# Splitting the value products of the grouped attention of a two-layer gated Flamingo kernel into three passes

## The chip, the cores and the metric

The kernel runs on one NeuronCore of a Trainium2 chip. It is written in Bass: every engine has a program of its own, which it executes in the order written, and the engines meet only at semaphores. TensorE does the matmuls, VectorE, ScalarE and GpSimd the element-wise work, SyncE issues the DMAs. The metric is the device time of one execution in microseconds (us), as the median of several runs.

## What is computed

The reference is a two-layer network over a batch of 8 sequences of 100 tokens with 256 features. The part that the change touches is the attention inside the second layer's feed-forward block: 32 query heads share 4 heads of keys and values, each 128 wide. Cut to that part:

```python
h = _rmsnorm(hidden_states, ln1_w)
q = (h @ Wq).reshape(B, S, NH, HD)          # NH = 32, HD = 128
k = (h @ Wk).reshape(B, S, KVH, HD)         # KVH = 4
v = (h @ Wv).reshape(B, S, KVH, HD)
q = _rope(q, pos)
k = _rope(k, pos)
k = jnp.repeat(k, rep, axis=2)              # rep = 8
v = jnp.repeat(v, rep, axis=2)
scores = jnp.einsum('bqhd,bkhd->bhqk', q, k) / jnp.sqrt(jnp.float32(HD))
scores = jnp.where(causal[None, None], scores, jnp.float32(-1000000000.0))
attn = jax.nn.softmax(scores, axis=-1)
o = jnp.einsum('bhqk,bkhd->bqhd', attn, v).reshape(B, S, NH * HD) @ Wo
x = resid + o
```

Here S is 100 and B is 8, so there are T = 800 tokens. All of it is in fp32.

## The kernel before, in words

The whole network runs as a row of stages in one launch, with a barrier of all engines between stages. The change lies in the stage of the grouped attention (ST_F in the code). The stages before it compute the first layer, the second layer's first attention and the norms; the stage behind it computes a norm, and then a mixture of experts.

The stage first makes keys and values (PE L2014 and L2019). ScalarE copies the values of each of the 8 sequences from PSUM to the tile `v2` (L1016), and VectorE rotates the keys. Then come 64 units of work. A unit v takes four heads and one sequence: it is 100 query rows by 4 x 100 keys, and its tiles in PSUM are one bank each. Four consecutive units take the same four heads over the four sequences of one half of the batch, eight take the eight heads of a group over one half, and so on over two halves and four groups.

The order of the work is written out by hand as one loop over steps s on every engine, each unit's pieces spread over several steps:

- TensorE, step s: scores of unit s (L2051 writes the mask, L2054 the four heads), the query block s + 6 (L2035 to L2037), an output product that began nine steps earlier (L2091 to L2093), the value product of unit s - 3 (L2073), and the turn (transpose) of the probabilities of unit s - 2 (L2064).
- VectorE, step s: maximum of unit s (L1488) and its subtraction into `d2` (L1492), the low part of the attention output of unit s - 4 (`o2l`, L1514), the sum of unit s - 1 and its reciprocal (L1498, L1500), the two products of the rotation of query block s + 6 (`q2`, L1477, and `qt`, L1481), and in two of eight steps an addition of an output to the residual `R` (L1506).
- ScalarE, step s: the exponential of unit s (L1029), two half copies of query block s + 6 with the halves swapped (`qsw`, L1024 and L1025), the copy of the attention output of unit s - 3 rounded to fp32r (`o2h`, L1047), the copy of the turned probabilities of unit s - 2 out of PSUM (`pt2`, L1036), and in some steps the rounded high part of a block of weights (L1057, L1065).
- GpSimd, step s: the normalisation of unit s - 1 (`p2`, L723), the sum that ends the rotation of query block s + 6 (L717), and in some steps the low part of a block of weights (`wql`, L729, and `wol`, L734).

Products of full precision are done in one of two ways. One is a matmul on fp32 operands, as the value product here. The other splits both operands into a part rounded to fp32r and a rest in fp32r, and sums three matmuls (high by high, high by low, low by high); queries and outputs are done so, and the function `split3` writes it:

```python
mm(out_, wh, mh, start=start, stop=False)
mm(out_, wh, ml, start=False, stop=False)
return mm(out_, wl, mh, start=False, stop=stop)
```

Buffers tie the engines together. The scores have two banks, the turned probabilities one (bank 2), the value product one (bank 3). So the value product of a unit waits until VectorE has made `o2l` of the unit before it, and the turn waits until the turned probabilities of the unit before have left bank 2. Query blocks live in a ring of ten.

Of the kernel before, what the change touches and what calls it, by code (L numbers as in the profile page):

```python
# [9 lines left out]
fp32 = mybir.dt.float32  # L10
fp32r = mybir.dt.float32r
bf16 = mybir.dt.bfloat16
u32 = mybir.dt.uint32
ALU = mybir.AluOpType
ACT = mybir.ActivationFunctionType
# [3 lines left out]
def flamingo(nc, a, out, scratch, sorted_x, sorted_y):  # L19

    P = 128
    B, S, D = a["ctx_T"].shape[0], a["rope_q"].shape[2], a["xT"].shape[0]
    T = B * S
    NC = D // P
    HALF = T // 2
    HB = B // 2
# [26 lines left out]
    G2 = a["L1_ffn_Wk"].shape[1] // P  # L53
    HG = NH2 // G2
    E1 = a["L1_ffn_Wg"].shape[0]
    U0 = B * NC
# [4 lines left out]
    with ctx:  # L61
        def sb(name, shape, dt=fp32, stack=ctx):
            return stack.enter_context(nc.sbuf_tensor(name, shape, dt))
# [6 lines left out]
        hT = sb("hT", [P, NC, T])  # L70
        xc = sb("xc", [P, NC, T])
        sq = sb("sq", [P, NC, T])
        rstd = sb("rstd", [P, T])
# [24 lines left out]
        PS = ctx.enter_context(nc.psum_tensor("PS", [P, 8, 512], fp32))  # L98
# [18 lines left out]
        def moe_memory(tag, stack):  # L117
# [62 lines left out]
        st2 = ExitStack()  # L180
# [9 lines left out]
        qlo = sb("qlo", [P, 2, HALF], fp32r, stack=st2)  # L190
# [21 lines left out]
        QRING = 10  # L212
# [3 lines left out]
        rope2 = sb("rope2", [P, 2, S], stack=st)  # L216
        st2 = ExitStack()
        kr = sb("kr", [P, G2, T], stack=st2)
        v2 = sb("v2", [S, B, G2 * P], stack=st2)
        wq2 = sb("wq2", [P, NC, HG * P], stack=st2)  # L220
        wo2 = sb("wo2", [P, HG, D], stack=st2)
        wqh = sb("wqh", [P, NC, HG * P], fp32r, stack=st2)
        wql = sb("wql", [P, NC, HG * P], fp32r, stack=st2)
        woh = sb("woh", [P, HG, D], fp32r, stack=st2)
        wol = sb("wol", [P, HG, D], fp32r, stack=st2)
        h1h = sb("h1h", [P, NC, T], fp32r, stack=st2)
        h1l = sb("h1l", [P, NC, T], fp32r, stack=st2)
        q2 = sb("q2", [P, QRING, HALF], stack=st2)
        qsw = sb("qsw", [P, 2, HALF], stack=st2)
        qt = sb("qt", [P, 2, HALF], stack=st2)  # L230
        d2 = sb("d2", [S, 3, 4, S], stack=st2)
        p2 = sb("p2", [S, 2, 4, S], stack=st2)
        pt2 = sb("pt2", [S, 2, 4 * S], stack=st2)
        mx2 = sb("mx2", [S, 2, 4], stack=st2)
        su2 = sb("su2", [S, 3, 4], stack=st2)
        sm2 = sb("sm2", [S, 3, 4], stack=st2)
# [31 lines left out]
        p0 = {k: sem(f"l0_{k}") for k in ("q", "k", "ke", "v", "ve", "kx", "o", "vz")}  # L268
        ATT = ("s", "mx", "sub", "exp", "sum", "rec", "norm", "t", "pte", "pv", "pve")
        at = {k: sem(f"att_{k}") for k in ATT}  # L270
# [10 lines left out]
        xa = {k: sem(f"xa_{k}") for k in ("rope", "f", "fe", "fd", "qh", "qhe", "qb", "rp", "rr", "qp",  # L281
                                          "qlo", "qhi", "qst")}
# [3 lines left out]
        fs = {k: sem(f"f_{k}") for k in ("ldk", "k", "kw", "kc", "ka", "v", "ve",  # L286
                                         "ldq", "ldo", "q", "qw", "qc", "qs", "qa", "o", "oa")}
        XQ = 2 * H1
        fs.update(hs=xa["qh"], wqh=xa["qhi"], wql=xa["qlo"], woh=xa["qhe"], wol=xa["qst"], ol=xa["qb"])
        done, stored = sem("done"), sem("stored")  # L290

        block = ctx.enter_context(nc.Block())
# [40 lines left out]
        U2, LEAD, BACK = 2 * B * G2, 6, 9  # L333
# [204 lines left out]
        def _(pool):  # L538
# [174 lines left out]
            def add_queries(n):  # L713

                pool.wait_ge(fs["qs"], n + 1)
                q = q2[:, n % QRING]
                pool.tensor_tensor(q, q, qt[:, n % 2], ALU.add).then_inc(fs["qa"], 1)  # L717

            def normalise2(v):
# [44 lines left out]
        def _(act):  # L764
# [248 lines left out]
                    act.activation(ksw[lo, n % 4], PS[hi, n, 0:HALF], ACT.Copy).then_inc(fs["kw"], 1)  # L1013
            for b in range(B):
                act.wait_ge(fs["v"], b + 1)
                act.activation(v2[:, b, :], PS[0:S, b, :], ACT.Copy).then_inc(fs["ve"], 1)  # L1016

            def swap_queries(n):

# [11 lines left out]
            def keep_turned2(v):  # L1031

                act.wait_ge(at["t"], U0 + v + 1)
                if v >= 2:
                    act.wait_ge(at["pv"], U0 + v - 1)
                act.activation(pt2[:, v % 2], PS[0:S, 2, 0:4 * S], ACT.Copy).then_inc(at["pte"], 1)  # L1036

            def keep_values2(v):

# [69 lines left out]
        def _(dve):  # L1109
# [204 lines left out]
            for u in range(2 * H1 + 2):  # L1314
# [12 lines left out]
                w = u - 2  # L1327
# [78 lines left out]
            for u in range(NU):  # L1406
                k = maximum(u)
            negative_maxima(0, k)
            maxima_rows(0)
            for b in range(B + 1):  # L1410
                for s in range(SP_ if b < B else 15):
# [4 lines left out]
                    if more:  # L1416
                        for u in range(UNITS[s], UNITS[s + 1]):
                            k = maximum(u)
# [37 lines left out]
            def split_inputs(h):  # L1456

                dve.tensor_copy(h1h[:, :, half(h)], h1[:, :, half(h)]).then_inc(fs["hs"], 1)
                dve.wait_ge(fs["hs"], XQ + 2 * h + 1)
                dve.tensor_tensor(h1l[:, :, half(h)], h1[:, :, half(h)], h1h[:, :, half(h)].bitcast(fp32),  # L1460
                                  ALU.subtract).then_inc(fs["hs"], 1)
            split_inputs(0)
            for n in range(2 * G2):
                k_ = kr[:, n // 2, half(n % 2)].rearrange("p (b s) -> p b s", s=S)
                w_, t_ = (t[:, n % 4].rearrange("p (b s) -> p b s", s=S) for t in (ksw, tk))
# [4 lines left out]
                dve.tensor_tensor(k_, t_, w_, ALU.add).then_inc(fs["ka"], 1)  # L1470

            split_inputs(1)

            def rotate_queries(n):

                dve.wait_ge(fs["qw"], 2 * n + 2)
                dve.tensor_tensor(q2[:, n % QRING].rearrange("p (b s) -> p b s", s=S),  # L1477
                                  PS[:, query_bank(n), 0:HALF].rearrange("p (b s) -> p b s", s=S), cq, ALU.mult).then_inc(fs["qc"], 1)
                if n >= 2:
                    dve.wait_ge(fs["qa"], n - 1)  # L1480
                dve.tensor_tensor(qt[:, n % 2].rearrange("p (b s) -> p b s", s=S), qsw[:, n % 2].rearrange("p (b s) -> p b s", s=S),  # L1481
                                  sn, ALU.mult).then_inc(fs["qs"], 1)
# [26 lines left out]
            def low_values2(v):  # L1509

                x, k, b = unit2(v)
                y = 2 * x + k
                dve.wait_ge(at["pve"], U0 + v + 1)
                dve.tensor_tensor(o2l[:, y % 3, :, b % HB, :], PS[:, 3, 0:4 * S].rearrange("p (h s) -> p h s", s=S),  # L1514
                                  o2h[:, y % 3, :, b % HB, :].bitcast(fp32), ALU.subtract).then_inc(fs["ol"], 1)
            for s in range(U2 + BACK + 2):
                if s < U2:
                    shift2(s)
                if 4 <= s < U2 + 4:
                    low_values2(s - 4)  # L1520
                if 1 <= s < U2 + 1:
                    inverse_sum2(s - 1)
                if s + LEAD < U2:
                    rotate_queries(s + LEAD)
                if s >= BACK + 6 and (s - BACK - 6) % HG in (0, 2):
                    add_outputs((s - BACK - 6) // HG, (s - BACK - 6) % HG // 2)
# [34 lines left out]
            for c in range(NC):  # L1561
                for h in range(2):
                    n = 2 * c + h
# [6 lines left out]
        def _(pe):  # L1570
            mm = pe.matmul
# [41 lines left out]
            for c in range(NC):  # L1613
                for h in range(2):
                    mm(PS[:, 4 + c * 2 + h, 0:HALF], wkv0T[:, c * P:(c + 1) * P], c0T[:, half(h)],
                       start=True, stop=True).then_inc(p0["k"], 1)
# [11 lines left out]
            for c in range(NC):  # L1628
                for h in range(2):
                    for i in range(NC):  # L1630
                        last = mm(PS[:, c * 2 + h, 0:HALF], wq0T[:, i, c * P:(c + 1) * P], hT[:, i, half(h)],
                                  start=(i == 0), stop=(i == NC - 1))
# [40 lines left out]
            for c in range(NC):  # L1673
                for h in range(2):
                    for i in range(NC):
                        last = mm(PS[:, c * 2 + h, 0:HALF], wo0T[:, i, c * P:(c + 1) * P], o0T[:, i, half(h)],
                                  start=(i == 0), stop=(i == NC - 1))
# [17 lines left out]
            for b in range(B - 1):  # L1695
                n = B - 1 - b
# [114 lines left out]
            def split3(out_, wh, wl, mh, ml, start, stop):  # L1811
# [4 lines that stand above are left out]
# [54 lines left out]
            for s in range(2 * H1 + 2):  # L1870
                if s < 2 * H1:
                    h, q = s // 2, s % 2
# [167 lines left out]
            def scores2(v):  # L2040

                x, k, b = unit2(v)
                if v == 0:
                    pe.wait_ge(fs["ve"], B)
                if v % HG == 0:
                    pe.wait_ge(fs["ka"], x + 1)
                if v % 4 == 0:
                    pe.wait_ge(fs["qa"], v + 4)
                if v >= 2:
                    pe.wait_ge(at["sub"], U0 + v - 1)  # L2050
                mm(PS[0:S, v % 2, 0:4 * S].rearrange("p (h s) -> p h s", s=S), identb[0:S, 0:S],  # L2051
                   causal[:, None, :].to_broadcast([S, 4, S]), start=True, stop=False)
                for j in range(4):
                    last_ = mm(PS[0:S, v % 2, j * S:(j + 1) * S], q2[:, (HG * x + 4 * k + j) % QRING, b % HB * S:(b % HB + 1) * S],  # L2054
                               kr[:, x // 2, toks(b)], start=False, stop=(j == 3))
                last_.then_inc(at["s"], 1)

            def turn2(v):

                pe.wait_ge(at["norm"], U0 + v + 1)  # L2060
                if v >= 1:
                    pe.wait_ge(at["pte"], U0 + v)
                for j in range(4):
                    last_ = pe.transpose(PS[0:S, 2, j * S:(j + 1) * S], p2[:, v % 2, j, :], ident[0:S, 0:S])  # L2064
                last_.then_inc(at["t"], 1)

            def values2(v):

                x, k, b = unit2(v)
                pe.wait_ge(at["pte"], U0 + v + 1)  # L2070
                if v >= 1:
                    pe.wait_ge(fs["ol"], XQ + v)
                mm(PS[:, 3, 0:4 * S], v2[:, b, x // 2 * P:(x // 2 + 1) * P], pt2[:, v % 2], start=True, stop=True).then_inc(at["pv"], 1)  # L2073

            def outputs2(x, j):

# [123 lines left out]
```

## Time and profile before

| | us |
|---|---|
| median of 3 runs | 1597.94 |
| lowest and highest of them | 1597.33 to 1600.22 |
| the profiled execution, its own time | 1592.69 |
| its span, first to last instruction | 1590.9 |
| TensorE busy in the span | 1476.1 (93%) |
| VectorE busy | 913.4 (57%) |
| ScalarE busy | 619.0 (39%) |
| GpSimd busy | 778.0 (49%) |

All durations below come from the profiled execution. Its time is the span and 1.8 us around it. In the views PE is TensorE, PEld its loading of weights (which overlaps matmuls), DVE VectorE, ACT ScalarE, POOL GpSimd and SP SyncE; an "idle before" names the instruction of another engine whose end released the waiting one. Instructions overlap on an engine: the time from one start to the next is the price that an instruction has in its queue, and can be shorter than its own duration.

### The profile page before, as it was taken

To read this page: it belongs to the slowest core of one execution; us is meant where nothing else is said; L and a number is where in the kernel's file an instruction comes from. 1 tells how busy PE (TensorE), PEld (TensorE's weight loads), DVE (VectorE), ACT (ScalarE), POOL (GpSimd) and SP (SyncE) were. 2 spreads that over 40 slices of the span, in tenths; PEclk is the share of its full clock that TensorE was granted. 3 is DMA by queue.
4 is the path that set the end of the run, shared out by engine and by line. 5 is a ranking of instruction groups with operands and counts; after the bars stand their busy time and mean duration, and the time that the engine had idled before them with its cause. 6 is when DMAs were issued, how large, how long until landed. Compare 5 with 4: busy or idle time off the path is not lost. (4 is left out here: it accounts for less than half of the span.)

```text
span 1590.9 us, 20767 instructions
## 1 busy us (share of the span) xinstructions
PE 1476.1 (93%) x7316; PEld 1108.4 (70%) x7316; DVE 913.4 (57%) x1581; ACT 619.0 (39%) x1116; POOL 778.0 (49%) x605
## 2 busy tenths in 40 slices
PE   7899999899978999999999998979999998899998
PEld 4687466544445766666666665657889887899998
DVE  1662111245556676796787854557778774444444
ACT  2332121133341344343342443356566653333333
POOL 3650102135554897787877855046475651333332
PEclk7896999699997999999999999789999999899999
DMA  8004111611001010110110000200110001344441
GB/s 301 1 1 146 51 44 41 212 48 49 1 8 53 33 57 3 55 57 2 56 57 1 20 1 1 82 27 1 54 43 12 27 1 41 105 122 121 121 121 51
DMA packets 60317, 88.61 MB, mean 56 GB/s; under 512 B 7556, under 2 KB 44612, under 8 KB 60230
## 3 DMA queue, kind: packets, MB, share of 16 engines
q1 hardware_dynamic: 59206, 85.82, 16.8%
q0 software_dynamic: 1024, 1.64, 0.4%
q8 instruction: 53, 0.87, 0.2%
q14 instruction: 34, 0.28, 0.1%
HBM read 81.92 MB, written 5.41 MB: 55 GB/s over the span
## 5 line engine op out<-in xcount | busy, mean ns | idle before, releaser
L966 ACT ACTIVATE prob<-PS 121x800 f32<-121x800 f32 x192 | 158.1, 838 | 256.2 <-PE PS L1949 253.3
L1349 DVE TENSOR_REDUCE mx<-PS 128x1 f32<-128x482 f32 (+1 forms) x312 | 186.0, 651 | 45.8 <-PE PS L1929 44.4
L619 POOL TENSOR_TENSOR e_wl<-e_wf,e_wh 128x768 fp32r<-128x768 f32 x33 | 71.8, 2174 | 174.0 <-ACT e_wh L882 151.8
L1928 PE MATMUL PS<-kth,qs 128*128 128x482 f32 (+1 forms) x312 | 129.6, 415 | 17.9 <-DVE mx L1349 10.2
L696 POOL TENSOR_TENSOR hT<-hT,prob 121x800 f32<-121x800 f32 x56 | 109.5, 1956 | 70.4 <-ACT prob L966 68.4
L1964 PE MATMUL PS<-prob,kvn 121*64 121x400 f32 (+1 forms) x768 | 136.1, 503 | 0.9 <-ACT prob L966 0.9
L696 POOL TENSOR_TENSOR xc<-xc,prob 121x800 f32<-121x800 f32 x56 | 117.1, 2091 | 17.9 <-ACT prob L966 12.5
L1929 PE MATMUL PS<-kl,qm 66*128 66x482 f32 (+1 forms) x312 | 123.6, 396 | 0.0
L1946 PE MATMUL PS<-qs,kth 128*121 128x400 f32 (+1 forms) x384 | 112.1, 374 | 7.9 <-DMA qm<-nml 4.8
L1949 PE MATMUL PS<-qm,kl 66*121 66x400 f32 (+1 forms) x384 | 104.4, 354 | 0.0
L1964 PEld LDWEIGHTS PS<-prob,kvn 121*64 121x64 f32 (+1 forms) x768 | 52.3, 137 | 71.2 <-issue 68.6
L1946 PEld LDWEIGHTS PS<-qs,kth 128*121 128x121 f32 (+1 forms) x384 | 66.0, 189 | 48.2 <-issue 23.8
L1292 DVE TENSOR_TENSOR e_aw<-e_sg,PS 128x400 f32<-128x400 f32 x64 | 36.6, 571 | 102.8 <-ACT e_sg L888 102.8
L1813 PE MATMUL PS<-e_hh,e_wh 128*128 128x400 f32 x264 | 93.4, 354 | 0.3 <-POOL e_wl L619 0.3
L1814 PE MATMUL PS<-e_hl,e_wh 128*128 128x400 f32 x264 | 92.2, 349 | 0.0
L1815 PE MATMUL PS<-e_hh,e_wl 128*128 128x400 f32 x264 | 91.7, 347 | 0.0
L723 POOL TENSOR_TENSOR p<-d,sm 100x400 f32<-100x400 f32 x64 | 54.6, 853 | 75.7 <-DVE sm L1500 74.9
L1928 PEld LDWEIGHTS PS<-kth,qs 128*128 128x128 f32 x312 | 61.6, 197 | 40.8 <-DVE mx L1349 26.3
L717 POOL TENSOR_TENSOR q<-q,qt 128x400 f32<-128x400 f32 x64 | 66.8, 1045 | 46.0 <-DVE qt L1481 46.0
L667 POOL TENSOR_TENSOR rr<-rp 96x400 f32<-96x400 f32 x32 | 32.9, 1028 | 109.2 <-DVE rp L1326 109.2
L888 ACT ACTIVATE e_sg<-PS 128x400 f32<-128x400 f32 x66 | 33.3, 505 | 130.1 <-PE PS L1815 130.1
L1949 PEld LDWEIGHTS PS<-qm,kl 66*121 66x121 f32 (+1 forms) x384 | 72.4, 189 | 0.8
(277 smaller groups left out, 3582.0 us busy)
## 6 DMA issues: line engine op xcount, KB each, us to landing
e_wb<-routing SPq DMA_DIRECT2D x32, 400.0 KB, 4.0
wgu<-in_L_ffn_gate_up_proj SPq DMA_DIRECT2D x8, 1024.0 KB, 13.6
krt<-in_ctx_T SPq DMA_DIRECT2D x8, 722.0 KB, 4.2
ksw<-in_ctx_Tswap SPq DMA_DIRECT2D x8, 722.0 KB, 5.8
wdn<-in_L_ffn_down_proj SPq DMA_DIRECT2D x8, 512.0 KB, 7.9
wq<-in_L_ffn_Wq SPq DMA_DIRECT2D x4, 1024.0 KB, 5.2
wo<-in_L_ffn_Wo SPq DMA_DIRECT2D x4, 1024.0 KB, 5.5
e_wf<-in_L_ffn_Wg SPq DMA_DIRECT2D x32, 128.0 KB, 2.2
```

The source lines that it names most:

```text
L619: pool.tensor_tensor(m["wl"][:, slot], m["wf"][:, slot], m["wh"][:, slot].bitcast(fp32), ALU.subtract).then_inc(ms["wlo"], 1)
L696: pool.tensor_tensor(acc, acc, prob[:, n % RING], ALU.add).then_inc(xb["ap"], 1)
L966: act.activation(prob[0:k, n % RING], PS[0:k, 2 * (n % 2):2 * (n % 2) + 2, 0:GC], ACT.Exp).then_inc(xb["ex"], 1)
L1349: dve.tensor_reduce(mx3[:, m, g:g + 1], PS[:, 4 + k % 3, 0:SEG[g][1]], AX.X, ALU.max).then_inc(xb["free"], 1)
L1813: mm(out_, wh, mh, start=start, stop=False)
L1814: mm(out_, wh, ml, start=False, stop=False)
L1815: return mm(out_, wl, mh, start=False, stop=stop)
L1928: mm(bank, qs[:, b].rearrange("p h s -> p (h s)")[:, cols], kth[:, b % 2, keys], start=True, stop=False)
L1929: mm(bank, qm2[:, b % 2, cols], kl2[:, b % 2, keys], start=False, stop=True).then_inc(xb["fill"], 1)
L1946: mm(PS[0:key_rows(t), 2 * (n % 2) + g, 0:GC], kth[:, b % 2, keys], qs[:, b, 8 * hp + 4 * g:8 * hp + 4 * g + 4].rearrange("p h s -> p (h s ...
L1949: last = mm(PS[0:key_rows(t), 2 * (n % 2) + g, 0:GC], kl2[:, b % 2, keys], qm2[:, b % 2, (2 * hp + g) * GC:(2 * hp + g + 1) * GC], start=F ...
L1964: last = mm(PS[g * DC:g * DC + DC, 7, 0:GC], kvn[0:key_rows(t), b % 2, t], prob[0:key_rows(t), n % RING, g], start=(t == 0), stop=(t == KT ...
```

## The change

The value product is done by `split3` in place of one fp32 matmul. For that the copy of the turned probabilities becomes the rounded high part (`pt2h`, still ScalarE's), and VectorE subtracts it from the PSUM bank to get the low part (`pt2l`, a new function `low_turned2`, which opens each of VectorE's steps from s = 3 on). TensorE's turn and value product wait for the low part (semaphore `ptl`) where they waited for the copy. The values are split once, ahead of the units: ScalarE's copies become `v2h`, and VectorE makes `v2l` by eight subtractions behind its work on the keys. The query ring and the two buffers beside it no longer have tiles of their own but lie in the buffers of the norms (`xc`, `sq`, `rstd`, `hT`), which this stage doesn't use otherwise.

```diff
--- before.py
+++ after.py
@@ -216,7 +216,8 @@
         rope2 = sb("rope2", [P, 2, S], stack=st)
         st2 = ExitStack()
         kr = sb("kr", [P, G2, T], stack=st2)
-        v2 = sb("v2", [S, B, G2 * P], stack=st2)
+        v2h = sb("v2h", [S, B, G2 * P], fp32r, stack=st2)
+        v2l = sb("v2l", [S, B, G2 * P], fp32r, stack=st2)
         wq2 = sb("wq2", [P, NC, HG * P], stack=st2)
         wo2 = sb("wo2", [P, HG, D], stack=st2)
         wqh = sb("wqh", [P, NC, HG * P], fp32r, stack=st2)
@@ -225,12 +226,13 @@
         wol = sb("wol", [P, HG, D], fp32r, stack=st2)
         h1h = sb("h1h", [P, NC, T], fp32r, stack=st2)
         h1l = sb("h1l", [P, NC, T], fp32r, stack=st2)
-        q2 = sb("q2", [P, QRING, HALF], stack=st2)
-        qsw = sb("qsw", [P, 2, HALF], stack=st2)
-        qt = sb("qt", [P, 2, HALF], stack=st2)
+        q2 = [t_[:, c, k * HALF:(k + 1) * HALF] for t_ in (xc, sq) for c in range(NC) for k in range(2)]
+        q2 += [rstd[:, k * HALF:(k + 1) * HALF] for k in range(2)]
+        qsw, qt = (hT[:, c].rearrange("p (k n) -> p k n", k=2) for c in range(NC))
         d2 = sb("d2", [S, 3, 4, S], stack=st2)
         p2 = sb("p2", [S, 2, 4, S], stack=st2)
-        pt2 = sb("pt2", [S, 2, 4 * S], stack=st2)
+        pt2h = sb("pt2h", [S, 2, 4 * S], fp32r, stack=st2)
+        pt2l = sb("pt2l", [S, 2, 4 * S], fp32r, stack=st2)
         mx2 = sb("mx2", [S, 2, 4], stack=st2)
         su2 = sb("su2", [S, 3, 4], stack=st2)
         sm2 = sb("sm2", [S, 3, 4], stack=st2)
@@ -286,7 +288,8 @@
         fs = {k: sem(f"f_{k}") for k in ("ldk", "k", "kw", "kc", "ka", "v", "ve",
                                          "ldq", "ldo", "q", "qw", "qc", "qs", "qa", "o", "oa")}
         XQ = 2 * H1
-        fs.update(hs=xa["qh"], wqh=xa["qhi"], wql=xa["qlo"], woh=xa["qhe"], wol=xa["qst"], ol=xa["qb"])
+        fs.update(hs=xa["qh"], wqh=xa["qhi"], wql=xa["qlo"], woh=xa["qhe"], wol=xa["qst"], ol=xa["qb"], ptl=xa["qp"], vh=p0["ke"])
+        XV = 4
         done, stored = sem("done"), sem("stored")
 
         block = ctx.enter_context(nc.Block())
@@ -713,7 +716,7 @@
             def add_queries(n):
 
                 pool.wait_ge(fs["qs"], n + 1)
-                q = q2[:, n % QRING]
+                q = q2[n % QRING]
                 pool.tensor_tensor(q, q, qt[:, n % 2], ALU.add).then_inc(fs["qa"], 1)
 
             def normalise2(v):
@@ -1013,7 +1016,7 @@
                     act.activation(ksw[lo, n % 4], PS[hi, n, 0:HALF], ACT.Copy).then_inc(fs["kw"], 1)
             for b in range(B):
                 act.wait_ge(fs["v"], b + 1)
-                act.activation(v2[:, b, :], PS[0:S, b, :], ACT.Copy).then_inc(fs["ve"], 1)
+                act.activation(v2h[:, b, :], PS[0:S, b, :], ACT.Copy).then_inc(fs["vh"], 1)
 
             def swap_queries(n):
 
@@ -1033,7 +1036,7 @@
                 act.wait_ge(at["t"], U0 + v + 1)
                 if v >= 2:
                     act.wait_ge(at["pv"], U0 + v - 1)
-                act.activation(pt2[:, v % 2], PS[0:S, 2, 0:4 * S], ACT.Copy).then_inc(at["pte"], 1)
+                act.activation(pt2h[:, v % 2], PS[0:S, 2, 0:4 * S], ACT.Copy).then_inc(at["pte"], 1)
 
             def keep_values2(v):
 
@@ -1470,11 +1473,14 @@
                 dve.tensor_tensor(k_, t_, w_, ALU.add).then_inc(fs["ka"], 1)
 
             split_inputs(1)
+            for b in range(B):
+                dve.wait_ge(fs["vh"], XV + b + 1)
+                dve.tensor_tensor(v2l[:, b, :], PS[0:S, b, :], v2h[:, b, :].bitcast(fp32), ALU.subtract).then_inc(fs["ve"], 1)
 
             def rotate_queries(n):
 
                 dve.wait_ge(fs["qw"], 2 * n + 2)
-                dve.tensor_tensor(q2[:, n % QRING].rearrange("p (b s) -> p b s", s=S),
+                dve.tensor_tensor(q2[n % QRING].rearrange("p (b s) -> p b s", s=S),
                                   PS[:, query_bank(n), 0:HALF].rearrange("p (b s) -> p b s", s=S), cq, ALU.mult).then_inc(fs["qc"], 1)
                 if n >= 2:
                     dve.wait_ge(fs["qa"], n - 1)
@@ -1513,7 +1519,15 @@
                 dve.wait_ge(at["pve"], U0 + v + 1)
                 dve.tensor_tensor(o2l[:, y % 3, :, b % HB, :], PS[:, 3, 0:4 * S].rearrange("p (h s) -> p h s", s=S),
                                   o2h[:, y % 3, :, b % HB, :].bitcast(fp32), ALU.subtract).then_inc(fs["ol"], 1)
+            def low_turned2(v):
+
+                dve.wait_ge(at["pte"], U0 + v + 1)
+                if v >= 2:
+                    dve.wait_ge(at["pv"], U0 + v - 1)
+                dve.tensor_tensor(pt2l[:, v % 2], PS[0:S, 2, 0:4 * S], pt2h[:, v % 2].bitcast(fp32), ALU.subtract).then_inc(fs["ptl"], 1)
             for s in range(U2 + BACK + 2):
+                if 3 <= s < U2 + 3:
+                    low_turned2(s - 3)
                 if s < U2:
                     shift2(s)
                 if 4 <= s < U2 + 4:
@@ -2051,7 +2065,7 @@
                 mm(PS[0:S, v % 2, 0:4 * S].rearrange("p (h s) -> p h s", s=S), identb[0:S, 0:S],
                    causal[:, None, :].to_broadcast([S, 4, S]), start=True, stop=False)
                 for j in range(4):
-                    last_ = mm(PS[0:S, v % 2, j * S:(j + 1) * S], q2[:, (HG * x + 4 * k + j) % QRING, b % HB * S:(b % HB + 1) * S],
+                    last_ = mm(PS[0:S, v % 2, j * S:(j + 1) * S], q2[(HG * x + 4 * k + j) % QRING][:, b % HB * S:(b % HB + 1) * S],
                                kr[:, x // 2, toks(b)], start=False, stop=(j == 3))
                 last_.then_inc(at["s"], 1)
 
@@ -2059,7 +2073,7 @@
 
                 pe.wait_ge(at["norm"], U0 + v + 1)
                 if v >= 1:
-                    pe.wait_ge(at["pte"], U0 + v)
+                    pe.wait_ge(fs["ptl"], XQ + v)
                 for j in range(4):
                     last_ = pe.transpose(PS[0:S, 2, j * S:(j + 1) * S], p2[:, v % 2, j, :], ident[0:S, 0:S])
                 last_.then_inc(at["t"], 1)
@@ -2067,10 +2081,11 @@
             def values2(v):
 
                 x, k, b = unit2(v)
-                pe.wait_ge(at["pte"], U0 + v + 1)
+                pe.wait_ge(fs["ptl"], XQ + v + 1)
                 if v >= 1:
                     pe.wait_ge(fs["ol"], XQ + v)
-                mm(PS[:, 3, 0:4 * S], v2[:, b, x // 2 * P:(x // 2 + 1) * P], pt2[:, v % 2], start=True, stop=True).then_inc(at["pv"], 1)
+                w = slice(x // 2 * P, (x // 2 + 1) * P)
+                split3(PS[:, 3, 0:4 * S], v2h[:, b, w], v2l[:, b, w], pt2h[:, v % 2], pt2l[:, v % 2], True, True).then_inc(at["pv"], 1)
 
             def outputs2(x, j):
```

## Rows read from the trace of the kernel before

**Rows 1.** Page, part 1; busy by stretch (PE, PEld, DVE, ACT, POOL), clock, DMA.

```profile
PE 1476.1 (93%) x7316; PEld 1108.4 (70%) x7316; DVE 913.4 (57%) x1581; ACT 619.0 (39%) x1116; POOL 778.0 (49%) x605
...
1080.00:1100.00 20.00, 16.57 (x111) 13.87 (x109) 16.69 (x35) 14.88 (x34) 14.00 (x18) 1.00 0.01 2
```

**Rows 2.** Groups by line in the attention stage: busy, mean | idle before, releaser.

```profile
L2091 PEld LDWEIGHTS PS<-o2h,woh 128*128 128x128 f32 x128 | 24.1, 188 | 11.7 <-POOL wol L734 11.6
```

**Rows 3.** TensorE's timeline, one steady step: start us, us, line, operation [idle before].

```profile
1143.27 0.34 PE L2093 MATMUL PS<-o2h,wol 128*128 128x400 f32 x1
1143.45 0.84 PE L2073 MATMUL PS<-pt,v 100*128 100x400 f32 x2
1144.13 0.50 PE L2064 MATMUL PS<-ident,p 100*100 100x100 f32 x4
1144.47 0.33 PE L2051 MATMUL PS<-causal,identb 100*100 100x400 bf16 x1
...
1148.57 0.33 PE L2051 MATMUL PS<-causal,identb 100*100 100x400 bf16 x1
```

**Rows 4.** VectorE's timeline, the same step.

```profile
1145.55 0.57 DVE L1488 TENSOR_REDUCE mx<-PS 100x4 f32<-100x400 f32 x1 [0.22 <-PE PS L2054]
1146.15 0.57 DVE L1492 TENSOR_TENSOR d<-PS,mx 100x400 f32<-100x400 f32 x1
1146.65 0.56 DVE L1514 TENSOR_TENSOR o2l<-PS,o2h 128x400 fp32r<-128x400 f32 x1
1147.13 0.56 DVE L1498 TENSOR_REDUCE su<-d 100x4 f32<-100x400 f32 x1
...
1148.38 0.57 DVE L1477 TENSOR_TENSOR q<-PS,rope 128x400 f32<-128x400 f32 x1 [0.48 <-ACT qsw L1025]
1148.88 0.57 DVE L1481 TENSOR_TENSOR qt<-qsw,rope 128x400 f32<-128x400 f32 x1
```

**Rows 5.** ScalarE's timeline, the same step.

```profile
1146.76 0.54 ACT L1029 ACTIVATE d<-d 100x400 f32<-100x400 f32 x1 [1.54 <-DVE d L1492]
1147.33 0.50 ACT L1024 ACTIVATE qsw<-PS 64x400 f32<-64x400 f32 x1
1147.85 0.50 ACT L1025 ACTIVATE qsw<-PS 64x400 f32<-64x400 f32 x1
...
1148.82 0.50 ACT L1036 ACTIVATE pt<-PS 100x400 f32<-100x400 f32 x1
```

**Rows 6.** VectorE's timeline, maxima of two early steps.

```profile
1063.45 0.57 DVE L1488 TENSOR_REDUCE mx<-PS 100x4 f32<-100x400 f32 x1
...
1067.24 0.57 DVE L1488 TENSOR_REDUCE mx<-PS 100x4 f32<-100x400 f32 x1
```

**Rows 7.** VectorE's timeline, a step that adds outputs to R.

```profile
1299.86 0.57 DVE L1488 TENSOR_REDUCE mx<-PS 100x4 f32<-100x400 f32 x1
...
1303.66 0.57 DVE L1506 TENSOR_TENSOR R<-R,PS 128x400 f32<-128x400 f32 x1
1304.14 0.57 DVE L1488 TENSOR_REDUCE mx<-PS 100x4 f32<-100x400 f32 x1
```

**Rows 8.** VectorE's timeline, the maximum of step 5.

```profile
1076.89 0.57 DVE L1488 TENSOR_REDUCE mx<-PS 100x4 f32<-100x400 f32 x1 [1.96 <-PE PS L2054]
```

**Rows 9.** Timelines of VectorE and TensorE around the second value product.

```profile
1071.05 0.57 DVE L1488 TENSOR_REDUCE mx<-PS 100x4 f32<-100x400 f32 x1
...
1072.14 0.56 DVE L1514 TENSOR_TENSOR o2l<-PS,o2h 128x400 fp32r<-128x400 f32 x1
...
1072.85 1.67 PE L2073 MATMUL PS<-pt,v 100*128 100x400 f32 x2 [2.75 <-DVE o2l L1514]
```

**Rows 10.** VectorE's timeline, the maximum of step 63.

```profile
1324.80 0.57 DVE L1488 TENSOR_REDUCE mx<-PS 100x4 f32<-100x400 f32 x1 [1.62 <-PE PS L2054]
```

**Rows 11.** Timelines of ScalarE and VectorE ahead of the first step.

```profile
1041.11 0.60 ACT L1016 ACTIVATE v<-PS 100x512 f32<-100x512 f32 x1 [1.12 <-PE PS L2019]
...
1045.41 0.57 DVE L1477 TENSOR_TENSOR q<-PS,rope 128x400 f32<-128x400 f32 x1 [12.21 <-ACT qsw L1025]
```

## The prediction

> **What bounds the kernel now.** I read the page first, then the costly groups by line inside the grouped attention, then the timelines of single engines there. The page shows TensorE busy for 93% of the span [rows 1], so the reader might expect any cheaper matmul to shorten the kernel. That share is an average; the change touches one stage late in the span, and its limit has to be read there. In its steady part one unit of attention (a step of the four queues) takes TensorE 4.11 us, from 1144.47 to 1148.57 us, without a pause [rows 3]. So TensorE sets the pace, but narrowly. Each unit's fp32 value product runs as two matmuls, and the next kind of matmul starts 0.68 us after their beginning [rows 3].
>
> The second thing to see is VectorE's round. Its queue holds, per step: maximum, subtraction, low part of the output, sum, reciprocal, and then the rotation of a query block, for which it waits 0.48 us on ScalarE's two half copies [rows 4]. Those copies stand behind the exponential in ScalarE's queue [rows 5], and the exponential waits for VectorE's subtraction of the same step. This closes a round: subtraction to exponential 0.61, to first copy 0.57, to second 0.52, to rotation 0.53, to its second product 0.50, to the next maximum 0.48, to the next subtraction 0.60: 3.81 us [rows 4, 5], where the 0.48 is the usual time from one start to the next, as from o2l to su. The trace also shows it bare: in the first steps of the stage, one runs from 1063.45 to 1067.24, 3.79 us [rows 6]. I use 3.80. So VectorE's 0.48 us of waiting isn't free room: it is time in which the round waits for itself, and only 4.11 - 3.80 = 0.31 us per step is spare.
>
> **The change, part by part.** *Value products.* Two fp32 passes (0.68 us) become three fp32r passes. fp32r matmuls over 400 columns start 0.18 us apart, as L2093 and the one behind it [rows 3], so 3 x 0.18 = 0.54: TensorE's step becomes 3.97 us, 0.14 less, 64 x 0.14 = 9 us of work. This counts only where TensorE sets the pace. Bound: at most some 0.1 more per unit where a pass follows a change of type or a wait, which the spare time of the new rhythm covers.
>
> *Low part of the turned probabilities.* VectorE gets 64 subtractions of 100 x 400, PSUM and SBUF in, fp32r out: the nearest row is o2l, 0.56 us long, its successor starting 0.48 us after it [rows 4]. It is queued between the query rotation and the next maximum, that is, inside the round: 3.80 + 0.48 = 4.28 us, above TensorE's 3.97. The trace of before shows exactly this price: in the steps in which VectorE adds outputs to R, one more such instruction stands at the same place, and the maxima lie 1304.14 - 1299.86 = 4.28 us apart [rows 7]; there the next step catches up, because the addition comes only in 2 of 8 steps. Now every step has it.
>
> The Trainium skill, "VectorE: DVE Perf Modes", section "The DRAIN you can't avoid", says that the next VectorE instruction doesn't start until the pipe of the one before is empty. By that the price would be the whole 0.56 us, some 53 x 0.08 = 4 us more in all; the rows, 0.48 us from one start to the next, disagree, and the sum goes by them.
>
> The subtraction waits for ScalarE's copy. The copy starts at 1148.82 and lasts 0.50 [rows 5], so it is there at 1149.32; behind the rotation (start 1148.88) VectorE comes to it at 1149.36 [rows 4]. That is just in time and can go wrong by 0.1 us per step, 53 x 0.1 = 5 us: the upper bound. Behind it wait the maximum and all of VectorE's step, and through the subtraction ScalarE's exponential. On TensorE the value product and the next turn now wait for the low part instead of the copy; behind them stand the next scores. VectorE makes it while TensorE still has that step's scores, queries and outputs ahead of it, so this wait ends before TensorE gets there.
>
> *Steps 5 to 58.* Before, the maximum of step 5 starts at 1076.89 and that of step 58 at 1304.14 [rows 7, 8]: 227.25 us for 53 steps. 53 x 4.11 is 217.8; the rest, 9.4, is mostly six stalls of some 1.5 us in which TensorE's output products wait for GpSimd's low output weights (11.6 us in the whole stage, with a seventh later) [rows 2]. After: 53 x 4.28 = 226.8; 12 steps with an addition to R, 12 x 0.48 = 5.8, of which three fall into a stall and are hidden (-1.4); six stalls, each shorter by TensorE's new spare time, 6 x (1.5 - 0.3) = 7.2, since GpSimd's weights are queued behind work that VectorE releases and stay late with it. Sum 238.4: **+11.1 us**.
>
> *Start.* Low parts 0 and 1 stand in front of maxima 3 and 4: twice 0.48 later. The second value product, at 1072.85, waits for the low output at 1072.14 [rows 9], which comes after those. The cheaper product there, at the lower clock, gives half back: **+0.5 us**.
>
> *End.* Steps 58 to 63 run from 1304.14 to 1324.80 [rows 7, 10] with no query rotation, so the round is shorter and the low part fits: 0. In the last three units nothing covers the way from the copy over the low part (0.53, as from the half copy to the rotation) to the product (0.71, as from o2l to the product [rows 9]), which was one hop before: some 0.7 each, 3 x 0.7 = **+2 us**; lower bound 0.
>
> *Values split once.* Eight copies on ScalarE stay as they were, the last starting at 1041.11; VectorE gets eight subtractions of 100 x 512, by o2l's rate some 0.65 each, 5.2 us. They lie in the 12.21 us in which VectorE waits before 1045.41 [rows 11], the last ready about 1042.4. A query block waits for the values of one bank alone, and the first of them only for the fifth of eight. Cost 0; if that cover were gone, up to 5 us. *Query ring in the norms' buffers:* the same instructions and shapes at other addresses, the norms being over: 0. No DMA is added or moved, and SP's queue is untouched.
>
> **Sum:** 11.1 + 0.5 + 2 = +13.6 us. The profiled execution took 1592.69 us, so the sum gives 1606.3 by its clock; the median of the runs is 1597.94, 5.25 above it, so I predict 1611.5 for the median.
>
> **Rivals.** *A, the other side: TensorE keeps the pace and the kernel gets faster.* If VectorE's waits were real room, the subtraction would vanish in them and some 48 steps would each fall by 0.14: -6.7 us, about 1591. It decides where the round without the new instruction is under 3.97 - 0.48 = 3.49 us. For it speaks that VectorE is idle some 0.7 us per step; against it the bare step of 3.79 [rows 6] and the 4.28 [rows 7]. Chance 0.07.
>
> *B, no difference.* The round grows by 4.28 - 4.11 = 0.17 us per step, but the stalls on weights vanish in TensorE's new spare time: 53 x 0.17 - 9 = 0 on the steps, with start and end some +2 us, 1600. Against it: GpSimd is released by VectorE, so its lateness moves along. Chance 0.08.
>
> *C, slower still.* The copy comes late by 0.1 us a step, or the instruction costs its full 0.56: +4 to +10 more, 1616 to 1621. Chance 0.15.
>
> *D, the clock.* With waits in every step TensorE's clock might fall to the lower level in the stalls. The product behind the 2.75 us wait took 1.67 us instead of 0.84, so it ran at the lower level, and the maxima around it lie 1076.89 - 1071.05 = 5.84 us apart [rows 3, 8, 9]. Six such falls at some 2 us each would give +12 more, 1624. Against it: from 1080 to 1100 us TensorE had no work for 17% of the time and the granted clock was 1.00 [rows 1], the higher of its levels, 2.4 GHz. The Trainium skill, "TensorE: Matmul & The Clock Gate", section "HAM oscillation — how this bites in real kernels", describes such falls behind waits in each pass of a loop. Chance 0.05.
>
> **How the numbers follow.** The forecast has 0.65: 1606 to 1616 by its own bounds. Range 1603 to 1621: it takes in the forecast and C and leaves out A, most of B and D, together a little under 0.2. A measurement of this kernel can tell about 0.2%, 3.2 us, from no change. Faster than that is A, 0.07; within it B, 0.08; slower by more the forecast, C and D, 0.85.
>
> **What would show it.** Right: in the new trace maxima 4.28 us apart in plain steps and 4.76 where R is added to; TensorE idle some 0.3 us per step before the value products, the releaser being VectorE's low output; three passes 0.18 us apart; low parts behind qt without an idle gap. Wrong: TensorE without pauses at 3.97 us per step (A), VectorE idle before the low part with ScalarE's copy as releaser (C), a granted clock under 1.00 in the steady part (D). The forecast falls if the round in plain steps isn't between 4.2 and 4.35 us.

## The result

The changed kernel takes 1610.37 us (median of 5 runs, 1607.85 to 1614.95), the kernel before 1597.33 us over its five runs. The ratio is 1.010, with a 95% interval of 1.0076 to 1.0124: slower by 13.0 us, about as forecast (1611.5).

The profile of the changed kernel, page, part 1, which answers to [rows 1]:

```profile
PE 1488.9 (92%) x7380; PEld 1125.8 (70%) x7380; DVE 938.1 (58%) x1653; ACT 618.7 (38%) x1116; POOL 778.7 (48%) x605
```

VectorE has 72 instructions more (64 low parts of probabilities, 8 of values), and TensorE 64 (three passes for two). Its profiled execution is the slowest of the five runs, 1614.95 us, and there the attention's first maximum already comes 7.6 us later than before. Of these, 6.0 us are there at the stage's first matmul (1014.82 us before, 1020.87 now), ahead of everything that was changed; 1.4 arise in the key products, which are the same instructions and ran at a mean granted clock of 0.79 instead of 0.87. 0.2 us come behind the last copy of the values. In the ten profiles of this study the first maximum comes between 1051.0 and 1066.8 us. So I compare the stretch that holds the 64 units: from the first maximum (VectorE, unit 0) to the end of the last addition to `R`. Before:

```profile
1055.57 0.57 DVE L1488 TENSOR_REDUCE mx<-PS 100x4 f32<-100x400 f32 x1
...
1340.76 0.57 DVE L1506 TENSOR_TENSOR R<-R,PS 128x400 f32<-128x400 f32 x1 [1.63 <-PE PS L2093]
```

Now:

```profile
1063.19 0.57 DVE L1494 TENSOR_REDUCE mx<-PS 100x4 f32<-100x400 f32 x1
...
1361.42 0.57 DVE L1512 TENSOR_TENSOR R<-R,PS 128x400 f32<-128x400 f32 x1 [1.62 <-PE PS L2108]
```

It took 1341.33 - 1055.57 = 285.8 us before and takes 1361.99 - 1063.19 = 298.8 us: 13.0 us more, as between the medians.

Three views of the changed kernel show where they are. First VectorE's timeline over one plain step, which answers to [rows 4]:

```profile
1232.33 0.57 DVE L1494 TENSOR_REDUCE mx<-PS 100x4 f32<-100x400 f32 x1
...
1235.15 0.57 DVE L1483 TENSOR_TENSOR sq<-PS,rope 128x400 f32<-128x400 f32 x1 [0.48 <-ACT hT L1028]
1235.64 0.56 DVE L1487 TENSOR_TENSOR hT<-hT,rope 128x400 f32<-128x400 f32 x1
1236.12 0.57 DVE L1527 TENSOR_TENSOR pt2l<-PS,pt2h 100x400 fp32r<-100x400 f32 x1
1236.61 0.57 DVE L1494 TENSOR_REDUCE mx<-PS 100x4 f32<-100x400 f32 x1
```

The two maxima are 4.28 us apart. The low part costs 1236.61 - 1236.12 = 0.49 us, and VectorE still waits its 0.48 us for ScalarE's half copies: that wait was never room. (The query ring and `qsw` and `qt` now bear the names of the norms' buffers, xc, sq, rstd and hT.)

Then TensorE's timeline in the same stretch, which answers to [rows 3]:

```profile
1233.72 0.34 PE L2108 MATMUL PS<-o2h,wol 128*128 128x400 f32 x1
1234.13 0.42 PE L1827 MATMUL PS<-pt2h,v2h 100*128 100x400 f32 x1
1234.39 0.34 PE L1828 MATMUL PS<-pt2l,v2h 100*128 100x400 f32 x1
1234.57 0.34 PE L1829 MATMUL PS<-pt2h,v2l 100*128 100x400 f32 x1
1234.76 0.51 PE L2078 MATMUL PS<-ident,p 100*100 100x100 f32 x4
```

The three passes take 0.63 us from their beginning to the turn, the first of them 0.26 behind a pause of some 0.2 us. So the product did become cheaper, and TensorE waits. The groups by line in the stage name what it waits for (busy, mean | idle before and releaser):

```profile
L2106 PE MATMUL PS<-o2h,woh 128*128 128x400 f32 x128 | 45.6, 356 | 11.2 <-POOL wol L737 11.2
...
L1527 DVE TENSOR_TENSOR pt2l<-PS,pt2h 100x400 fp32r<-100x400 f32 x64 | 36.5, 570 | 15.6 <-ACT pt2h L1039 15.6
...
L1827 PE MATMUL PS<-pt2h,v2h 100*128 100x400 f32 x64 | 26.8, 418 | 20.4 <-DVE o2l L1520 15.9 <-DVE pt2l L1527 2.8
```

The product waits for the low output (15.9 us), as foreseen, and hardly for the low part (2.8). TensorE's waits for GpSimd's weights stay and have grown: six of 1.25 us and one of 1.65 before are six of 1.50 and one of 1.92 now, with a small one behind them. The first of the six, in TensorE's timelines before and now:

```profile
1099.55 0.45 PE L2091 MATMUL PS<-o2h,woh 128*128 128x400 f32 x1 [1.25 <-POOL wol L734]
```

```profile
1107.20 0.45 PE L2106 MATMUL PS<-o2h,woh 128*128 128x400 f32 x1 [1.50 <-POOL wol L737]
```

VectorE's own wait for ScalarE's copy isn't spread over the steps: the timeline shows it in the steps behind those stalls and in the last units.

### The profile page after: what moved, and what is told of

Same layout as the page of the kernel before. It is cut to its first block and busy times, and to the rows that moved or that the text cites. A ratio compares the mean times of both kernels' runs of the same rounds, so it can differ in the third digit from the quotient of the medians.

```text
span 1613.2 us, 21029 instructions
## 1 busy us (share of the span) xinstructions
PE 1488.9 (92%) x7380; PEld 1125.8 (70%) x7380; DVE 938.1 (58%) x1653; ACT 618.7 (38%) x1116; POOL 778.7 (48%) x605
## 5 line engine op out<-in xcount | busy, mean ns | idle before, releaser
L699 POOL TENSOR_TENSOR xc<-xc,prob 121x800 f32<-121x800 f32 x56 | 116.5, 2080 | 21.6 <-ACT prob L969 15.9
L1032 ACT ACTIVATE d<-d 100x400 f32<-100x400 f32 x64 | 34.4, 538 | 103.2 <-DVE d L1498 103.2
```

The source lines that it names most:

```text
L699: pool.tensor_tensor(acc, acc, prob[:, n % RING], ALU.add).then_inc(xb["ap"], 1)
```

## The experiments

The stretch is from the first maximum to the end of the last addition to `R`, from each kernel's one profile. The ratio is that of its runs to those of the kernel before on the same chip.

| kernel | stretch, us | ratio (95%) |
|---|---|---|
| before | 285.8 | |
| changed | 298.8 | 1.010 (1.0076 to 1.0124) |
| e1, no low part | 281.6 | 0.9995 (0.997 to 1.0019) |
| e2, fp32 product | 300.8 | 1.0138 (1.01 to 1.0175) |
| e3, low part later | 299.5 | 1.0099 (1.0071 to 1.0127) |
| e4, both orders | 286.9 | 1.0043 (1.0022 to 1.0063) |
| e5, scores first only | 318.1 | one run, 1631.6 us |
| e10, no collision | 277.3 | 0.9972 (0.995 to 0.9994) |
| e11, weights earlier | 267.5 | 0.9892 (0.9859 to 0.9925) |
| e9, before, reordered | 267.7 | 0.991 (0.9876 to 0.9945) |

**e1: the passes without the subtraction.**

```diff
-                split3(..., pt2h[:, v % 2], pt2l[:, v % 2], True, True)
+                split3(..., pt2h[:, v % 2], pt2h[:, v % 2], True, True)
-                if 3 <= s < U2 + 3:
-                    low_turned2(s - 3)
```

This kernel leaves the low part of the probabilities out, and TensorE waits for the copy again, as before the change.

> Three fp32r passes stay, VectorE's 64 subtractions per unit go (the second pass reads the high part again, so the low part of the probabilities is left out and the high product counts twice). Theory (VectorE's round is lengthened by the subtraction): the round is back at 3.80 us, TensorE's 3.97 sets the pace, steady steps 3.97 instead of 4.28, and the kernel is some 6 us faster than before, about 1591 us. Rival (the three passes or the wait behind them on TensorE cost the time): steps stay near 4.28, time 1605 us or more.

VectorE's timeline of e1, two maxima of neighbouring steps:

```profile
1202.95 0.57 DVE L1494 TENSOR_REDUCE mx<-PS 100x4 f32<-100x400 f32 x1
...
1206.94 0.57 DVE L1494 TENSOR_REDUCE mx<-PS 100x4 f32<-100x400 f32 x1
```

3.99 us, and the stretch is 4.2 us shorter than before. In the stretch the three passes alone save time; the 17 us to the changed kernel's stretch belong to the subtraction and TensorE's wait for it. The query ring still lies in the norms' buffers here, so its new place isn't what costs. In the whole time the expected 6 us don't show: the ratio can't be told from no change, nor from the stretch's 4.2 us.

**e2: the subtraction without the passes.** The tiles of the high parts become fp32, and the product is one matmul:

```diff
-                split3(...)
+                mm(PS[:, 3, 0:4 * S], v2h[:, b, w], pt2h[:, v % 2], start=True, stop=True)
```

> The subtraction and its waits stay where the change put them, the product is one fp32 matmul again. Theory: the round of 4.28 us is above TensorE's 4.11, so steps stay at 4.28 and the time at some 1610 to 1613 us. Rival (the three passes cost the time): steps back at 4.11 and 1597 us.

```profile
1232.33 0.57 DVE L1494 TENSOR_REDUCE mx<-PS 100x4 f32<-100x400 f32 x1
...
1236.62 0.57 DVE L1494 TENSOR_REDUCE mx<-PS 100x4 f32<-100x400 f32 x1
```

Its maxima, in VectorE's timeline, are 4.29 us apart, though the product is back at its old price. Stretch 300.8 us, 2.0 more than with the passes. e1 and e2 together show that the step's length hangs on the subtraction and not on the product; that it is its place in VectorE's queue, and not TensorE's wait for it, e5 tells.

**e3: the low part behind the low output.**

```diff
                 if s < U2:
                     shift2(s)
                 if 4 <= s < U2 + 4:
                     low_values2(s - 4)
+                if 3 <= s < U2:
+                    low_turned2(s - 3)
```

The three steps behind the last unit keep it in front.

> The changed kernel with one piece moved: VectorE makes the low part behind the low output instead of ahead of the maximum. Theory: the exponential's round is back at 3.80, but another round takes over, since the value product waits for the low part and the next scores are queued behind it: maximum to subtraction 0.60, to low output 0.49, to low part 0.48, to product 0.71, three passes 0.54, turn 0.35, scores to maximum 1.08: 4.25 us. Plain steps 4.25, steps with an addition to R no longer 4.76 but about 4.28: some 4 to 5 us less than the changed kernel, 1605 us. Rival 1 (only the amount of VectorE's work counts): no change, 1610 us. Rival 2 (the place ahead of the maximum alone was at fault): steps 3.97, 1591 us.

The plain step is 4.27 us, as worked out for the second round; by time alone this could not be told from "no change". The groups by line of e3 tell it:

```profile
L1487 DVE TENSOR_TENSOR hT<-hT,rope 128x400 f32<-128x400 f32 x64 | 55.6, 869 | 0.9 <-POOL xc L720 0.9
...
L1829 PE MATMUL PS<-pt2h,v2h 100*128 100x400 f32 x64 | 28.1, 439 | 20.0 <-DVE pt2l L1527 17.3 <-DVE o2l L1520 2.1
```

Now the product waits for the low part, 17.3 us where the changed kernel had 2.8: the round through TensorE has taken the place of the one through ScalarE. The expected 4 to 5 us from the steps with an addition didn't come: those take 4.60, not 4.28. The first row says why: the second rotation product has become slower, 0.87 us instead of 0.61. So the kernel is no faster than the changed one (1.0099 against 1.010) where 4 to 5 us were expected. Rival 2, that the place alone was at fault, falls.

**e5: TensorE's order alone.**

```diff
-                if s < U2:
-                    scores2(s)
+                if s == 0:
+                    scores2(0)
...
+                if s + 1 < U2:
+                    scores2(s + 1)
                 if 3 <= s < U2 + 3:
                     values2(s - 3)
```

> The changed kernel with TensorE's order alone moved (scores of unit s + 1 ahead of the value product of unit s - 3); VectorE's low part stays ahead of the maximum. Theory: VectorE's round of 4.28 us with ScalarE doesn't pass over TensorE's order, so plain steps stay at 4.28. Rival (the product with its new wait, queued ahead of the scores, is what lengthens the step): plain steps about 3.97.

Plain steps stay at 4.28 us, in VectorE's timeline of e5:

```profile
1230.41 0.56 DVE L1494 TENSOR_REDUCE mx<-PS 100x4 f32<-100x400 f32 x1
...
1234.70 0.56 DVE L1494 TENSOR_REDUCE mx<-PS 100x4 f32<-100x400 f32 x1
```

TensorE's wait for the low part no longer stands ahead of the next scores, and the step is no shorter: the round over ScalarE sets it. But the steps with a stall grow from 5.0 to 5.5 us to between 7.3 and 8.9, which I hadn't expected (this rests on one run). TensorE's timeline of e5 there:

```profile
1104.54 0.60 PE L2106 MATMUL PS<-o2h,woh 128*128 128x400 f32 x1 [2.37 <-POOL wol L737]
1104.94 0.54 PE L2107 MATMUL PS<-o2l,woh 128*128 128x400 f32 x1
1105.27 0.54 PE L2108 MATMUL PS<-o2h,wol 128*128 128x400 f32 x1
```

The wait is 2.37 us instead of 1.50, and behind it the passes are 0.33 us apart instead of 0.18: the lower level of the clock. From 1100 to 1120 us the granted clock was 0.91 on the mean. This is rival D, brought about by another order; in the changed kernel itself the clock stayed at 1.00 from 1100 to 1360 us.

**e4: both orders**, that is e3's and e5's edits together.

> As the one before, and TensorE makes the scores of unit s + 1 ahead of the value product of unit s - 3 instead of behind the turn. Theory: neither round holds the low part any more, TensorE's 3.97 or VectorE's own work (3.80, 4.28 with an addition) sets the pace: about 1590 us, faster than before. Rival 1 (the amount of VectorE's work counts): 1610 us. Rival 2 (the passes on TensorE are the price): 1605 us or more.

Plain steps are 4.11 us: better than 4.28, but not 3.97, and the kernel is 0.43% slower than the one before, where faster was expected. VectorE's timeline of e4:

```profile
1213.83 0.58 DVE L1483 TENSOR_TENSOR xc<-PS,rope 128x400 f32<-128x400 f32 x1
1214.32 0.87 DVE L1487 TENSOR_TENSOR hT<-hT,rope 128x400 f32<-128x400 f32 x1
1215.12 0.56 DVE L1494 TENSOR_REDUCE mx<-PS 100x4 f32<-100x400 f32 x1
```

and GpSimd's in the same stretch:

```profile
1213.91 0.85 POOL L726 TENSOR_TENSOR p<-d,sm 100x400 f32<-100x400 f32 x1 [1.70 <-DVE sm L1506]
```

VectorE waits for nothing any more; its queue has become the bound. The 0.87 us product reads two SBUF tiles while GpSimd's normalisation runs from 1213.91 to 1214.76, and it ends 0.43 us behind that, at 1215.19. Rows with a PSUM operand beside it keep their 0.56 to 0.58.

**e10: e4 with the low part behind the reciprocal**, which then comes 0.48 us earlier and releases GpSimd earlier.

> As the kernel with both orders moved, but VectorE makes the low part behind the reciprocal instead of ahead of the sum. In that kernel VectorE had no idle time left and the second rotation product, SBUF by SBUF, took 0.87 us instead of 0.56 while GpSimd's normalisation ran. The reciprocal that releases GpSimd now comes 0.48 earlier, so the normalisation (0.85) should be over when that product starts. Theory (the two got into each other's way): the product is back at 0.56 us, VectorE's step at 3.80, TensorE's 3.97 sets the pace, plain steps 3.8 to 4.0; from the first maximum to the last addition to R some 281 us instead of 286.9; time some 5 us under before. Rival (VectorE's queue is full for another reason): plain steps stay at 4.11.

```profile
L1487 DVE TENSOR_TENSOR hT<-hT,rope 128x400 f32<-128x400 f32 x64 | 39.0, 610 | 1.0 <-POOL xc L720 1.0
```

In the groups by line the product is back at 0.61 us on the mean, 0.56 in the plain steps. These take 3.80 to 4.02 us, those around an addition 4.2 to 4.8, those around a stall on the weights 4.4 to 4.9. The stretch is 277.3 us, 8.5 less than before, and the ratio is 0.9972: some 4 us faster, with an interval that only just leaves out no change.

**e11: e10 with the output weights split one step earlier.**

```diff
-            g, n = (s - 5) // (2 * HG), (s - 5) % (2 * HG)
+            g, n = (s - 4) // (2 * HG), (s - 4) % (2 * HG)
```

> As the one before, and the output weights are split one step earlier (ScalarE and GpSimd). Theory: the six stalls in which TensorE waits for GpSimd's low output weights go, 6 x 1 to 1.5 us: from the first maximum to the last addition to R 272 to 275 us, time some 12 us under before. Rival (the stalls only move to the next late work of GpSimd): 278 us or more.

```profile
L2108 PE MATMUL PS<-o2h,woh 128*128 128x400 f32 x128 | 44.9, 351 | 0.0
```

The wait for low weights is gone (0.0 in the groups by line), and the stretch is 267.5 us, even below the 272 to 275 expected. With 1573.02 us and a ratio of 0.9892 it is 1.1% faster than the kernel before, with the three passes in it.

**e9: the kernel before with e5's and e11's edits**, fp32 products.

> The kernel before the change, fp32 products, with the scores ahead of the value product and the output weights one step earlier. It tells what the three passes are worth once the orders are right. Theory: TensorE's 4.11 sets the pace without stalls: plain steps 3.8 to 4.11, from the first maximum to the last addition to R 270 to 276 us, within 3 us of the kernel with three passes, since the 0.14 per unit saved on TensorE is spent on VectorE's queue. Rival (the passes are worth their 9 us of TensorE time): 6 to 9 us slower than that kernel.

Its stretch, in VectorE's timeline:

```profile
1053.36 0.57 DVE L1488 TENSOR_REDUCE mx<-PS 100x4 f32<-100x400 f32 x1
...
1320.51 0.57 DVE L1506 TENSOR_TENSOR R<-R,PS 128x400 f32<-128x400 f32 x1 [1.62 <-PE PS L2093]
```

That is 267.7 us, and the ratio is 0.991: within 1 us of e11 in the stretch, 1.6 in the median. So the gain comes from the scores ahead of the value product and the earlier weights, which e9 does not tell apart, and the three passes with their subtraction are worth nothing that these runs can tell, for or against.

**What stays open.** In the whole time e2 and e4 lie some 6 to 7 us further above the kernel before than in the stretch (e4: +0.43%, 6.9 us, against 286.9 - 285.8 = 1.1). The stages ahead of the attention vary by more than that: in the six profiles whose instructions are the same up to the first maximum (changed, e3, e4, e5, e10, e11) it comes between 1053.7 and 1063.2 us. Whether a kernel's other edits move them was not tried.

## Why the prediction was right

The forecast and its mechanism held, and its parts nearly so. That the sum came within 0.6 us (13.0 against 13.6) is in part luck: the steps cost 0.9 more than worked out, the start 1.4 less.

- **The round.** Plain steps were to be 4.28 us and are 4.28; with an addition to `R` 4.76, and are 4.76 or 4.77. e1 and e2 show that it is the subtraction.
- **Steps 5 to 58.** +12.0 instead of +11.1, from the maxima of steps 5 and 58:

```profile
1083.65 0.57 DVE L1494 TENSOR_REDUCE mx<-PS 100x4 f32<-100x400 f32 x1
...
1322.86 0.57 DVE L1494 TENSOR_REDUCE mx<-PS 100x4 f32<-100x400 f32 x1
```

  That is 239.2 us, against 238.4 worked out. A step with a stall takes 5.51, 1.23 more than a plain one, against 1.5 before and 1.2 assumed: it shrank as worked out, though TensorE's wait in it grew from 1.25 to 1.50. (The prediction's 11.6 us is the wait of the weight loads; the matmuls waited 9.2 us in all.) Two of the six stalls, behind an addition, take only 5.03 and 5.04: there an addition is hidden. The sum had three hidden; the third is in step 58, behind this stretch.
- **Start, wrong in its step.** +0.5 was forecast; the first five steps took 1083.65 - 1063.19 = 20.5 us against 21.3 before, -0.9. The forecast had TensorE's long wait stand ahead of the second value product, as before. Now it stands ahead of the first, for the low part, and the second waits 0.20 us:

```profile
1075.22 0.70 PE L1827 MATMUL PS<-pt2h,v2h 100*128 100x400 f32 x1 [2.82 <-DVE pt2l L1527]
...
1081.17 0.49 PE L1827 MATMUL PS<-pt2h,v2h 100*128 100x400 f32 x1 [0.20 <-DVE o2l L1520]
```

  Behind the long wait TensorE again ran at the lower level (0.50 from 1075 to 1080 us), but VectorE's longer round covers that: step 4 took 4.28 us, not 5.84.
- **Steps 58 to 63.** 20.5 us against 20.7: 0 was forecast.
- **End.** +2 was forecast; from the maximum of unit 63 to the last addition it takes 18.6 us against 16.5: +2.1. In the last three units VectorE waits for the copy before each low part, 0.76 to 1.42 us at a time:

```profile
1352.83 0.57 DVE L1527 TENSOR_TENSOR pt2l<-PS,pt2h 100x400 fp32r<-100x400 f32 x1 [1.42 <-ACT pt2h L1039]
```

- **Values split once.** No cost was forecast, and none shows. The eight subtractions fall into VectorE's pause; it waits for the next work again behind them:

```profile
1049.16 0.69 DVE L1478 TENSOR_TENSOR v2l<-PS,v2h 100x512 fp32r<-100x512 f32 x1 [1.02 <-ACT v2h L1019]
1053.66 0.57 DVE L1483 TENSOR_TENSOR xc<-PS,rope 128x400 f32<-128x400 f32 x1 [3.81 <-ACT hT L1028]
```

- **The price of one instruction.** The rows' 0.48 us from start to start held (0.49 measured) and not the whole 0.56. By the rule that the prediction takes from the Trainium skill ("VectorE: DVE Perf Modes", section "The DRAIN you can't avoid"), that the next instruction waits for an empty pipe, the step would have been 4.36. But the same paragraph of the Trainium skill adds that a next instruction that is not held starts earlier; with that the trace agrees, and the prediction left it out.
- **The copy just in time (rival C).** In plain steps it is: the copy runs from 1235.55 to 1236.05, and the low part starts at 1236.12 with no idle time noted. C's wait appears in the stalls and in the last units alone.

```profile
1235.55 0.50 ACT L1039 ACTIVATE pt2h<-PS 100x400 fp32r<-100x400 f32 x1
```

Rival A fell with plain steps of 4.28 us, B because TensorE's waits for the weights did not vanish, and D isn't seen in the changed kernel's steady part.

## What to carry to other kernels

An idle wait on an engine is room only if the wait doesn't depend on that engine's own next work: follow the releaser back, and where the chain returns to the same engine a step earlier, its sum is the least time of a step, and an instruction put into it is paid in full. Where in the queue the instruction stands decides: behind the work that releases the other engine it can be nearly free (e10's plain steps take 3.8 to 4.0 us with it), but then look for the next round that it lengthens. A cheaper product on the busiest engine, paid for with work in such a round, made this kernel slower; with the orders changed the kernel gained as much without it.

## What the runs showed of the hardware

- VectorE's product of two SBUF tiles takes 0.56 us alone and 0.87 beside GpSimd's SBUF work, while subtractions and products with a PSUM operand keep 0.56 to 0.58 in the same stretch. Its end tells more than its length: in e4 it ends 0.42 to 0.45 us behind GpSimd's normalisation in each step in which the two overlap, and ahead of the units, where it takes 1.13 us (1054.35 to 1055.48 in the kernel before), 0.43 behind GpSimd's sum, which ends at 1055.05. So it looks held until GpSimd's instruction is over, not slowed. An edit that only moved the queue by half a microsecond set this collision off (e3, e4) and another removed it (e10).
- An fp32r pass behind a pause or behind matmuls of another type starts its successor later than 0.18 us: 0.26 in the plain step (1234.13 to 1234.39), 0.29 behind a stall (1107.20 to 1107.49). So the three passes were 0.63 us and not 0.54.
- The changed kernel's waits of 1.50 us left TensorE's granted clock at 1.00; e5's of 2.36 and 2.37 were each followed by passes at half speed, at once or within some 1.5 us. The length of the wait alone doesn't tell: behind one of e4's waits of 2.26 us the clock fell (0.79 from 1167 to 1175 us), behind the two others (1098.72 and 1238.76) it stayed at 1.00.
